# Edge attention on one core: the row numbers of the far gathers are copied a pass earlier

## The reference

```
xc, xn = x[row], x[col]                       # row = src, col = dst
h      = relu(xc @ W1[:d] + xn @ W1[d:] + b1)
mask   = sigmoid(h @ W2 + b2)                 # one number for each edge
agg    = segment_sum(mask * xn, row) / segment_sum(mask, row)
out    = relu((0.5 x + 0.5 agg) @ Wl + bl)    # x alone where a node has no edge
```

## Time and profile before

| | |
|---|---|
| Median of three runs | 4384.71 us |
| Profiled execution: time / span | 4387.37 / 4385.7 us |
| Mean granted TensorE clock | 0.876 of full speed |
| Busy over the span: PE / DVE / ACT / POOL | 82% / 73% / 49% / 35% |
| Edge attention, from its first plan load to the last addition | about 2720 to 4299 us |

### The profile page before, as it was taken

How to read it: one execution, slowest core, us unless ns; L and a number is a source line. 1 busy time by engine, 2 the same in 40 slices (tenths; PEclk the granted TensorE clock), 3 DMA queues, 4 the chain that set the end, 5 groups by cost and what they waited for, 6 DMA issues and landing times. The chain is left out here.

```text
span 4385.7 us, 95324 instructions
## 1 busy us (share of the span) xinstructions
PE 3589.6 (82%) x20539; PEld 2449.5 (56%) x20540; DVE 3189.3 (73%) x13027; ACT 2150.5 (49%) x6722; POOL 1552.8 (35%) x1256
## 2 busy tenths in 40 slices
PE   4868882798889999986997996888888888888884
PEld 2367781333333444433444445777787777777773
DVE  8899997798888888863003006888888888888885
ACT  0078893366767888862002004444444444444444
POOL 0068873000000000001011002776777777777760
PEclk8855555799999999997998998999999999999996
DMA  2011112001111222215874872444444444444451
GB/s 46 1 10 15 16 17 79 18 34 47 68 72 77 93 94 94 102 78 211 304 248 188 305 270 89 140 136 138 136 139 136 139 139 135 140 135 139 137 133 36
DMA packets 236581, 496.86 MB, mean 113 GB/s; under 512 B 52663, under 2 KB 153166, under 8 KB 236350
## 3 DMA queue, kind: packets, MB, share of 16 engines
q1 hardware_dynamic: 170017, 345.58, 23.3%
q0 software_dynamic: 66336, 149.10, 12.5%
HBM read 390.62 MB, written 103.93 MB: 113 GB/s over the span
## 5 line engine op out<-in xcount | busy, mean ns | idle before, releaser
L1676 POOL DMA_INDIRECT xs<-edge_table,ea_row_stage x1088 | 1103.6, 1014 | 463.3 <-issue 307.8
L1842 PE MATMUL ea_psa<-xs,slot_dst 128*128 128x129 f32 x3264 | 456.3, 284 | 239.7 <-DVE agg_t L1756 238.2
L1842 PEld LDWEIGHTS ea_psa<-xs,slot_dst 128*128 128x128 f32 x3264 | 413.7, 194 | 274.0 <-DVE agg_t L1756 265.5
L1231 PE MATMUL a_agg_ps<-a_adj_ring,parts 128*128 128x512 f16 (+1 forms) x2548 | 522.7, 368 | 47.6 <-DMA a_adj_ring<-adjacency 47.5
L1876 ACT ACTIVATE slot_dst<-ea_onehot,ea_mask 128x128 f32<-128x128 f16 x1632 | 535.3, 399 | 13.2
L1030 PE MATMUL ab_agg_ps<-ab_adj_stage,parts 128*128 128x512 f16 x1911 | 532.6, 389 | 0.0
L1756 DVE TENSOR_TENSOR agg_t<-agg_t,ea_psa 128x129 f32 x1632 | 462.9, 284 | 84.3 <-PE ea_psa L1842 69.3
L1870 ACT ACTIVATE ea_mask<-ea_dot,b 128x4 f32<-128x4 f32 x408 | 121.3, 297 | 807.7 <-DVE slot_src L1782 806.3
L448 ACT ACTIVATE dst_step<-iota,dst_low_bias 128x128 f16<-128x128 f16 x1188 | 358.4, 403 | 217.0 <-PEq L473 214.1
L428 POOL DMA_INDIRECT records<-both_parts,record_row x98 | 346.9, 3539 | 313.8 <-ACT both_parts L454 289.5
L1371 POOL TENSOR_TENSOR parts<-xs,parts 128x896 f16<-128x896 f32 x7 | 13.2, 1881 | 1227.9 <-ACT parts L1365 1227.9
(11 more groups left out here) (379 smaller groups left out, 6528.2 us busy)
## 6 DMA issues: line engine op xcount, KB each, us to landing
a_adj_ring<-adjacency SPq DMA_DIRECT2D x182, 896.0 KB, 4.6
ea_low_rows<-low_rows SPq DMA_DIRECT2D x411, 128.0 KB
adjacency<-ab_adj_stage SPq DMA_DIRECT2D x91, 512.0 KB, 2.6
adjacency<-ab_adj_stage SPq DMA_DIRECT2D x91, 384.0 KB, 2.3
ea_near_rows<-near_rows SPq DMA_DIRECT2D x137, 128.0 KB
xs<-edge_table,ea_row_stage POOLq DMA_INDIRECT x1088
edge_table<-vx SPq DMA_DIRECT2D x12, 512.0 KB, 2.9
records<-zero_rows SPq DMA_DIRECT2D x4, 840.0 KB, 10.2
```

What stands on the lines that cost most here:

```text
L1231: ins = nc.tensor.matmul(ps[:, h, 0:width], lhs(r, t), ring[:, g % SLOTS, k * DB:k * DB + width], start=t == 0 and r == 0, stop=t == NT - ...
L1676: nc.gpsimd.indirect_dma_start(got[:, h, g, k, 0:ROW], None, m.table, bass.IndirectOffsetOnAxis(ap=row_s[:, h, g, k:k + 1], axis=0)).then_ ...
L1842: ins = nc.tensor.matmul(psa[:, home, k, 0:AW], hot_m[:, g, k, :], what, start=True, stop=True)
```

## The change

The row numbers are no longer copied for both groups at the start of step t for pass t+1. Instead each group's are copied for pass t+2 right behind that group's `z` in step t. At that point the gathers of pass t, which used the same home `row_s[h][g]`, have landed. The plan row becomes 36 wide: columns 32 and 33 hold the first columns of the far groups two passes on, written by two further DMAs in `plan_edges`. VectorE loads 18 values per step where it loaded 16. Ahead of the first step the rows of passes 0 and 1 are both staged, and 6 values are loaded where 4 were. GpSimd's program, with its waits, is untouched.

```diff
+STEP_W = 36
...
-        none = sb("none", [P, 2 * 32], I32)
+        none = sb("none", [P, 2 * STEP_W], I32)
...
             sp.dma_start(rows_of(0, 28, 31), plan[:, :, 16:19]).then_inc(s_put, 16)
-            sp.wait_ge(s_put, 64)
+            sp.dma_start(rows_of(0, 32, 34)[:, 0, :], plan[:, 1, 16:18]).then_inc(s_put, 16)
+            sp.dma_start(rows_of(1, 32, 34)[0:TURNS - 1, 0, :], plan[1:TURNS, 0, 16:18]).then_inc(s_put, 16)
+            sp.wait_ge(s_put, 96)
...
-    m.plan = nc.dram_tensor("plan_rows", [PLAN_ROWS, 32], I32).ap()
+    m.plan = nc.dram_tensor("plan_rows", [PLAN_ROWS, STEP_W], I32).ap()
...
-        steps = sb("steps", [1, 2, 32], I32)
+        steps = sb("steps", [1, 2, STEP_W], I32)
...
-            def stage_rows(base, h):
-                for g in FAR:
-                    c = nc.s_assert_within(base[g], 0, SC, skip_runtime_bounds_check_because="the plan holds columns")
-                    nc.vector.tensor_copy(row_s[:, h, g, :], row_of[:, bass.ds(c, G)]).then_inc(s_rows, 1)
+            def stage_rows(base, h, g):
+                c = nc.s_assert_within(base, 0, SC, skip_runtime_bounds_check_because="the plan holds columns")
+                nc.vector.tensor_copy(row_s[:, h, g, :], row_of[:, bass.ds(c, G)]).then_inc(s_rows, 1)
...
-                v = load(dve, 1 - h, 16, 16)
+                v = load(dve, 1 - h, 16, 18)
                 dve.sem_inc(s_read, 1)
                 base = v[12:15]
-                stage_rows(base, 1 - h)
                 one_hots(base, t, 1 - h, seen)
...
                         nc.vector.tensor_tensor(z[:, g, :, :], psz[:, g, :, :], got[:, h, g, :, 0:D], ALU.add).then_inc(s_z[g], 1)
+                        stage_rows(v[16 + g], h, g)
                         adds[0]()
...
-            base = load(dve, 0, 28, 4)
+            base = load(dve, 0, 28, 6)
             dve.sem_inc(s_read, 1)
-            stage_rows(base, 0)
+            for g in FAR:
+                stage_rows(base[g], 0, g)
+            for g in FAR:
+                stage_rows(base[4 + g], 1, g)
             one_hots(base, 0, 0, 0)
```

## The result

The changed kernel takes 4436.45 us (median of four runs, 4430.67 to 4440.87) against 4384.80 for the kernel before (four runs). That is a ratio of 1.0113, with a 95% interval from 1.0101 to 1.0125: slower by some 50 us, where I had forecast 4386 us and a range that ended at 4410. Two later groups of runs gave 1.0113 and 1.0118 again.

What follows compares the result with a forecast made beforehand. VectorE's chain through `near_x` bounds 89 passes and TensorE's sums 45, never GpSimd. Gather waits -7.7, load and copies +7.4, plan DMAs +1.1, first load +0.1 sum to +0.9 us: 4386 us, range 4373 to 4410.

Steps and rivals of the forecast that it cites:

- I take 0.124, the slope between the two rows: VectorE's step load: 18 values cost 0.124 us more than 16, at 62 ns a value; bounds 0.03 and 0.36 us.
- Only the 89 passes count: Edge attention: load and copy delays cost only passes where VectorE waits for `near_x`, 7.4 us in all.
- the 45 passes' better start: First-half passes among the 89: moving the copies saves 0.08 us at the step's start, leaving net +0.044 us each.
- the other 45 passes: Passes where VectorE waits for TensorE's sums, 1.5 us each; the delay was to vanish into that wait.
- one of my own signs of being wrong: The forecast is wrong if the count of passes that wait for TensorE changes by over ten.
- GpSimd's wait and its lead: Edge attention: GpSimd's 138.1 us wait for row-number copies goes, gathers land 2.4 us earlier, and TensorE ends GpSimd's idle time.
- the eight: Gather waits of `z` behind GpSimd hiccups (idle about 2.03 us instead of 0.30): all go, gaining 5.3 us.
- the ninth: Gather wait in the last but one pass, 3.47 us: the lead takes 2.4 us of it.
- Plan DMAs, first load, contention: Two plan DMAs at 0.5 us each; first load delays the first gather 0.1; gathers beside one-hots 0, ±6 us.
- my 1.1 us: Two more plan DMAs, on the path at the stage's end: 0.5 us each and 0.05 between; bounds 0.5 and 1.9.
- The load falls into two instructions: Rival: VectorE's load splits, costing up to 0.36 us a pass instead of 0.124; about 4410 us; chance 0.20.
- GpSimd is the bound after all: Rival: VectorE's waits are consequences of late gathers, so passes shrink by 0.2 us, 27 us in all: 4359 us; chance 0.10.

Runs made afterwards that it cites:

- second profile of the kernel before: Kernel before with twenty extra, unused register loads ahead of VectorE's first step; the trace held only its usual 138 loads: 4391.5 us, single run.
- With 16 values: Changed kernel loading 16 values a step as before, so the copies behind each `z` take the wrong pass's row numbers: 4387.1 us, ratio 0.9993.
- move alone: Changed kernel with the load of 16 values as before, copies moved but gathering rows of the wrong pass: ratio 0.9993 to the kernel before.
- old order with short loads: Kernel before, copies still at the step's start, its load split into 4, 8 and 8 values, the eights behind the far sums: 4354.07 us, ratio 0.9933.
- its relatives with other loads: Changed kernel with its load split into 16 and 4, 4 and 16, 4, 12 and 4, or 4, 8 and 8 values: ratios 0.9382, 0.9318, 0.9307, 0.9336.

## Why the prediction was wrong

**The failed step: "I take 0.124, the slope between the two rows", with its bounds of 0.03 and 0.36 us.** The load term of the sum was mis-sized. Two more values cost 0.467 us a step, outside both bounds. The upper bound was a whole second load of four, 0.358; two left-over values cost more than that. The trace of before had a row that pointed there and that I did not read: one value costs 313 ns, where the line through 4 and 16 gives 172. A value outside a four has a price of its own, and a straight line between two multiples of four was a guess about a third kind.

```profile
L1653 DVEq TENSOR_LOAD <-pairs x1: 313/313/313, 2752.2 to 2752.2; - x1
```

**"Only the 89 passes count" failed as well.** With 0.467 in its place the load's term would have been 89 x 0.467 less the 0.08 us of the 45 passes' better start, 38 us; it measured 48.6. I had let the other 45 passes hide the delay in VectorE's wait for TensorE (65.8 us). That wait did not shrink; it is 70.5 us after, in 58 passes instead of 45, which was one of my own signs of being wrong. Compared place by place with the second profile of the kernel before, the 86 passes that waited for `near_x` in the kernel before grew by 0.32 us each and the 41 that waited for TensorE by 0.36. The likely reason, read from the kernel and not tested: TensorE's lookups and sums follow VectorE's one-hots and additions.

**GpSimd's wait and its lead: right in kind and size.** The wait for the copies went from 138.1 to 1.8 us. With 16 values the fourth gather of a pass ended 8.97 us ahead of the far sum (median of 110 passes) where it had been 6.55: 2.4 us of lead, as forecast; in the changed kernel, with its longer passes, 9.82. GpSimd's idle time is now put down to its issue for the most, and to TensorE's sums for only 54.6 us, where I had forecast TensorE.

**The gather waits: the eight right, the ninth wrong.** All eight behind the hiccups are gone, and the 134 passes won 4.6 to 5.1 us by the move where I had counted 5.3. For the ninth, in the last pass but one, I let the lead take 2.4 us. But there the gathers themselves are slow to land, and an earlier issue did not help: the end of the walk became 7.0 us longer. My sum had no term for that, and its cause is open.

**Plan DMAs, first load, contention.** The issues of the two new DMAs took 0.56 and 0.25 us where I took 0.5 each; the walk's first load stands at 2720.5 us in both profiles, so nothing of my 1.1 us shows. The first load took 841 ns for 358, 0.5 us where I took 0.1. A one-hot takes 419 ns in the median (422 before); no contention showed.

**The terms as measured.** +48.6 us for the load, -5.1 for the gather waits, +7.0 at the end, and 0.6 at the start of the walk: 51.1 us, for the +0.9 of my sum. Each is a difference of single profiles, known to some 2 us.

**The rivals.** "The load falls into two instructions" came nearest, but not by its mechanism: there is one instruction, 138 of them, and it is dearer than two would have been (0.467 against 0.36 us). "GpSimd is the bound after all" is not true of this kernel (move alone 0.9993). In the old order with short loads the same move is worth 30 us, but most of that goes with the granted clock, and about the rest with the waits behind the hiccups.

## What to carry to other kernels

A register load is priced by fours from a column that is a multiple of four: count the fours and the left-over values, pad 18 to 20, and ask for a row of the very size before drawing a line through two others. Take at the head of a step only what its first instructions need, and issue the rest behind an instruction of the engine that is longer than the load. A move that is worth nothing now can be worth 0.7% once that is done; read the granted clock before you say by what. A wait of two engines for each other did not absorb a delay here. And compare the last passes of a loop on their own: they can lose what the others win.

## What the runs showed of the hardware that I had not expected

- Loads into VectorE's registers, from the row's start: 1 value 309 ns, 4 in 359, 6 in 823, 8 in 600, 15 in 1546, 16 in 1103, 18 in 1576, 20 in 1356, 24 in 1602; four from the second, third or fourth column 974, 959 and 958, eight from the second 1841.
- The last gathers of the walk land late, and the end of the walk is 7 to 8 us longer in every kernel with the 36-column plan row and the right rows. In the changed kernel, from GpSimd's last gather to the last far sum it takes 18.4 us instead of 7.8, with the DMA engines 89% busy at 77 GB/s, where 46% gave 131 GB/s some passes before.
- The same kernel took 4383.4 and 5027.6 us on one chip at two times. All the difference was in edge attention, where signals of TensorE reached ScalarE and VectorE some 4 us later, and the order of the copies decided over 6% of the time. Whether this is the gathers' traffic, the fetching of instructions or something else, no run here tells; nor was the changed kernel itself measured in it, only its relatives with other loads (0.931 to 0.938).
